# A residual with weights chosen per batch: 4 MB transfers in a ring of four rooms, channel-major weights, one loop per engine

## The reference

```
W = weights[condition]                      # (64, 128, 128)
out = x + einsum('bct,bcd->bdt', x, W)      # for each batch: out = x + W^T x
```

## Time and profile before

| | |
|---|---|
| median of 3 runs | 325.06 us (324.98 to 325.37) |
| profiled execution | 324.97 us, its span 323.2 us |
| TensorE, VectorE, GpSimd busy | 240.3, 146.6, 19.0 us |
| moved by the DMA engines | 135.30 MB, mean 419 GB/s |
| granted clock of TensorE, mean | 0.928 |

### The profile page before, as it was taken

One profiled execution on the slowest core, in us unless ns is written; L12 is line 12 of the kernel. 1 busy time (PEld: TensorE's weight loads), 2 busy tenths in 40 slices (PEclk: granted clock), 3 DMA queues, 4 the chain that ended last, 5 costly groups with the idle time before them and its releaser, 6 DMA issues.

```text
span 323.2 us, 2326 instructions
## 1 busy us (share of the span) xinstructions
PE 240.3 (74%) x512; PEld 101.3 (31%) x512; DVE 146.6 (45%) x64; ACT 0.2 (0%) x1; POOL 19.0 (6%) x69
## 2 busy tenths in 40 slices
PE   0029999999999986867996869866688786878000
PEld 0014444444444432322342323322233332333000
DVE  0003766766757752555173552543545254553200
ACT  0000000000000000000000000000000000000000
POOL 0011100101001000000010000000000000000000
PEclk9999999999999998999597997999899798899755
DMA  7999999999999999999999999999999999999996
GB/s 279 382 414 422 422 425 429 428 424 430 426 428 430 425 431 426 427 431 426 429 428 427 430 425 428 430 425 430 428 427 430 426 429 428 426 430 426 429 430 284
DMA packets 17940, 135.30 MB, mean 419 GB/s; under 512 B 1042, under 2 KB 1042, under 8 KB 1554
## 3 DMA queue, kind: packets, MB, share of 16 engines
q10 hardware_dynamic: 9234, 68.16, 49.9%
q1 hardware_dynamic: 8704, 67.11, 49.7%
HBM read 68.16 MB, written 67.11 MB: 419 GB/s over the span
## 4 chain that ended last, share of the span: by engine, by line
DMA 69%; PE 20%; DVE 2%; issue 1%; ACTq 0%; POOLq 0%; DVEq 0%; ACT 0%; SPq 0%; POOL 0%
DMA out<-x_ring 59%; PE product L114 20%; DMA weight_table<-weights 6%; DMA x_ring<-x 5%; DVE x_ring L138 2%; POOLq L90 0%; ACTq L147 0%; ACTq L145 0%; DVEq L138 0%; ACT weight_table L149 0%; ACTq L144 0%; SPq L72 0%; POOLq L92 0%; SPq L84 0%; POOLq L97 0%
## 5 line engine op out<-in xcount | busy, mean ns | idle before, releaser
L114 PE MATMUL product<-x_ring,chosen_weights 128*128 (+1 forms) x512 | 240.3, 629 | 58.6 <-POOL chosen_weights L92 23.2
L138 DVE TENSOR_TENSOR x_ring<-product,x_ring 128x2048 f32 x64 | 146.6, 2291 | 154.7 <-PE product L114 154.7
L114 PEld LDWEIGHTS product<-x_ring,chosen_weights 128*128 128x128 f32 x512 | 101.3, 201 | 196.7 <-issue 196.7
L92 POOL COPY chosen_weights<-weight_table 128x128 f32 x64 | 18.8, 293 | 243.1 <-issue 125.2
L149 ACT MOVE_SHAPE weight_table<-weights x1 | 0.2, 160 | 1.4 <-PEq L166 1.4
L166 POOL MEMSET const-float32-0.0<- 128x1 f32 x1 | 0.1, 98 | 0.1
L166 POOL MEMSET const-bfloat16-1.0<- 128x1 bf16 x1 | 0.1, 101 | 0.0
L166 POOL MEMSET const-uint8-127<- 128x1 uint8 x1 | 0.1, 101 | 0.0
L166 POOL MEMSET const-float32-1.0<- 128x1 f32 x1 | 0.1, 98 | 0.0
L166 POOL BASE_LOAD x1 | 0.0, 17 | 0.2 <-issue 0.2
## 6 DMA issues: line engine op xcount, KB each, us to landing
x_ring<-x SPq DMA_DIRECT2D x32, 2048.0 KB, 16.3
out<-x_ring ACTq DMA_DIRECT2D x32, 2048.0 KB, 38.6
condition_row<-condition ACTq DMA_DIRECT2D x1, 0.2 KB
weight_table<-weights ACTq DMA_DIRECT2D x1, 0.5 KB, 18.8
```

Of the source, the lines that this page charges most:

```text
L92: pool.tensor_copy(chosen_weights[b][:, :], weight_table[:, bass.ds(state * features, features)]).then_inc(weights_chosen, 1)
L114: last = pe.matmul(product[:, b % psum_slots, m * BANK_COLUMNS:(m + 1) * BANK_COLUMNS], chosen_weights[b][:, :], x_ring[:, bass.ds(ring_co ...
L138: dve.tensor_tensor(tile, product[:, b % psum_slots, :], tile, AluOpType.add).then_inc(sum_done, 1)
```

## The change

The unit of transfer becomes four batches (4 MB). The ring keeps its size and has 4 rooms of 32 KB per partition (2 turns of 2), so two loads and two stores may be in flight. The weights array is transposed on the host to (channel, state, feature), so that each channel's 8 KB lie in one piece; ScalarE issues this load ahead of the condition row. The written-out first turns go: semaphores are given starting amounts instead. `room_free` takes the place of `out_stored`, `psum_free` that of `sum_done`, and a new `weights_free` is raised by VectorE once it has seen a product done; GpSimd waits for it before it overwrites a buffer of chosen weights. The core of the diff:

```diff
-BATCHES = 2
-STEPS = 4
+GROUP = 4
+IN_FLIGHT = 2
 RING_TURNS = 2
...
-            for u in range(STEPS):
-                load(0, u)
-
-            with sp.Fori(1, RING_TURNS) as turn:
-                for u in range(STEPS):
-                    sp.wait_ge(x_loaded[u], 16 * turn)
-                    load(turn, u)
-            with sp.Fori(RING_TURNS, turns) as turn:
-                for u in range(STEPS):
-                    sp.wait_ge(x_loaded[u], 16 * turn)
-                    sp.wait_ge(out_stored[u], 16 * (turn - RING_TURNS + 1))
-                    load(turn, u)
+            for g in range(IN_FLIGHT):
+                sp.sem_inc(x_loaded[g], 16)
+                sp.sem_inc(room_free[g], 16 * RING_TURNS)
+            with sp.Fori(0, turns) as turn:
+                for g in range(IN_FLIGHT):
+                    sp.wait_ge(x_loaded[g], 16 * (turn + 1))
+                    sp.wait_ge(room_free[g], 16 * (turn + 1))
+                    sp.dma_start(ring_group(turn, g), dram_group(x, turn, g)
+                                 ).then_inc(x_loaded[g], 16)
...
-                    pool.wait_ge(product_done, (turn - 1) * (STEPS * BATCHES) + b + 1)
-                    choose(turn, b)
+            pool.sem_inc(weights_free, per_turn)
+            with pool.Fori(0, turns) as turn:
+                for b in range(per_turn):
+                    pool.wait_ge(weights_free, turn * per_turn + b + 1)
...
+            dve.sem_inc(psum_free, psum_slots)
             with dve.Fori(0, turns) as turn:
...
+                    dve.wait_ge(product_done, turn * per_turn + b + 1)
+                    dve.sem_inc(weights_free, 1)
                     dve.tensor_tensor(tile, product[:, b % psum_slots, :], tile,
-                                      AluOpType.add).then_inc(sum_done, 1)
+                                      AluOpType.add).then_inc(psum_free, 1)
...
             act.dma_start(condition_row[0:1, :], condition.rearrange("(o b) -> o b", o=1)
                           ).then_inc(condition_loaded, 16)
-            act.dma_start(weight_table[:, :].rearrange("c (s d) -> c s d", s=states),
-                          weights.rearrange("s c d -> c s d")).then_inc(table_loaded, 16)
...
+            with act.Fori(0, turns) as turn:
+                for g in range(IN_FLIGHT):
+                    act.wait_ge(room_free[g], 16 * (turn + RING_TURNS))
+                    act.wait_ge(psum_free, turn * per_turn + (g + 1) * GROUP + psum_slots)
+                    act.dma_start(dram_group(out, turn, g), ring_group(turn, g)
+                                  ).then_inc(room_free[g], 16)
...
-        "weights": np.ascontiguousarray(L0_cond_weights),
+        "weights": np.ascontiguousarray(np.asarray(L0_cond_weights).transpose(1, 0, 2)),
```

More of the change, by code:

```diff
@@ L26, in conditioned_residual @@
     batches, channels, time = x.shape
-    states, _, features = weights.shape
-    turns = batches // (STEPS * BATCHES)
-    group = BATCHES * time
+    _, states, features = weights.shape
     matmuls = time // BANK_COLUMNS
     psum_slots = PSUM_BANKS // matmuls
+    per_turn = IN_FLIGHT * GROUP
+    turns = batches // per_turn
+    group_columns = GROUP * time
     with ExitStack() as ctx:
@@ L48, in conditioned_residual, with ring_column, ring_group, dram_group @@
         table_loaded = sem("table_loaded")
-        x_loaded = [sem(f"x_loaded{u}") for u in range(STEPS)]
-        out_stored = [sem(f"out_stored{u}") for u in range(STEPS)]
+        x_loaded = [sem(f"x_loaded{g}") for g in range(IN_FLIGHT)]
+        room_free = [sem(f"room_free{g}") for g in range(IN_FLIGHT)]
+        weights_free = sem("weights_free")
         weights_chosen = sem("weights_chosen")
         product_done = sem("product_done")
[L54 to L65, removed]
+        psum_free = sem("psum_free")
+        def ring_column(turn, g):
+            return (turn % RING_TURNS) * (IN_FLIGHT * group_columns) + g * group_columns
+        def ring_group(turn, g):
+            return x_ring[:, bass.ds(ring_column(turn, g), group_columns)].rearrange(
+                "c (b t) -> c b t", b=GROUP)
+        def dram_group(tensor, turn, g):
+            return tensor[bass.ds(turn * per_turn + g * GROUP, GROUP)].rearrange("b c t -> c b t")
         block = ctx.enter_context(nc.Block())
@@ L70, in _ @@
         def _(sp):
-            def load(turn, u):
-                sp.dma_start(ring_group(turn, u), batches_of(x, turn, u)).then_inc(x_loaded[u], 16)
-            for u in range(STEPS):
-                load(0, u)
-            with sp.Fori(1, RING_TURNS) as turn:
-                for u in range(STEPS):
-                    sp.wait_ge(x_loaded[u], 16 * turn)
-                    load(turn, u)
-            with sp.Fori(RING_TURNS, turns) as turn:
-                for u in range(STEPS):
-                    sp.wait_ge(x_loaded[u], 16 * turn)
-                    sp.wait_ge(out_stored[u], 16 * (turn - RING_TURNS + 1))
-                    load(turn, u)
+            for g in range(IN_FLIGHT):
+                sp.sem_inc(x_loaded[g], 16)
+                sp.sem_inc(room_free[g], 16 * RING_TURNS)
@@ L96, in _ @@
             pool.wait_ge(condition_loaded, 16)
             pool.wait_ge(table_loaded, 16)
[L98 to L101, removed]
-                    pool.wait_ge(product_done, (turn - 1) * (STEPS * BATCHES) + b + 1)
-                    choose(turn, b)
+            pool.sem_inc(weights_free, per_turn)
+            with pool.Fori(0, turns) as turn:
+                for b in range(per_turn):
+                    pool.wait_ge(weights_free, turn * per_turn + b + 1)
+                    state = pool.value_load(condition_row[0:1, bass.ds(turn * per_turn + b, 1)],
+                                            min_val=0, max_val=states - 1)
+                    pool.tensor_copy(chosen_weights[b][:, :],
+                                     weight_table[:, bass.ds(state * features, features)]
+                                     ).then_inc(weights_chosen, 1)
@@ L106, in _ @@
         @block.tensor
         def _(pe):
[L108 to L128, removed]
+            with pe.Fori(0, turns) as turn:
+                for b in range(per_turn):
+                    g, within = divmod(b, GROUP)
+                    if within == 0:
+                        pe.wait_ge(x_loaded[g], 16 * (turn + 2))
+                    pe.wait_ge(weights_chosen, turn * per_turn + b + 1)
+                    pe.wait_ge(psum_free, turn * per_turn + b + 1)
+                    for m in range(matmuls):
+                        last = pe.matmul(
+                            product[:, b % psum_slots, m * BANK_COLUMNS:(m + 1) * BANK_COLUMNS],
+                            chosen_weights[b][:, :],
+                            x_ring[:, bass.ds(ring_column(turn, g) + within * time + m * BANK_COLUMNS,
+                                              BANK_COLUMNS)],
+                            start=True, stop=True)
+                    last.then_inc(product_done, 1)
@@ L157, in _ @@
-            for u in range(STEPS):
-                act.wait_ge(out_stored[u], 16 * turns)
+            with act.Fori(0, turns) as turn:
[4 more added lines that the diff above has]
+                                  ).then_inc(room_free[g], 16)
+            for g in range(IN_FLIGHT):
+                act.wait_ge(room_free[g], 16 * (turns + RING_TURNS))
```

16 lines of the change are left out of this document (7 added, 9 removed).

## The result

The changed kernel took 329.5 us in the median of 4 runs (328.56 to 330.60), the kernel before 325.22: a ratio of 1.0123, 95% interval [1.0102, 1.0144].

A forecast was written before the change was run, and what follows sets the result against it. The DMA engines, pushing 135.3 MB plus losses at both ends, were taken as the bound. With -2.1 us weights, -1.8 trickle and +5.3 idle, span 324.6 plus 1.8 outside gave 326.4 us against 325.0; range 322.8 to 329.6.

The forecast's parts named there:

- an idle stretch ahead of a lone last store: Near the end: DMA engines stand idle from 308.6 to 313.9 us, 5.3 us, before the last 4 MB store runs alone.
- rival 3: Middle: four rooms are too few, so the load stream pauses in every group; 329.2 us, chance 0.09.
- Weights, -2.1 us: Start: channel-major weights with 8 KB runs give back the whole 2.1 us lost at 377 GB/s; bounds 0 and 2.1.
- Rival 2: Start: the weights bring nothing and everything behind shifts by 2.1 us; 328.5 us, chance 0.09.
- TensorE's start 15.5 us: Start: TensorE's first matmul moves from 21.84 to 15.5 us, which by itself buys nothing.
- First store issued 34.6, first packet 38.2: First group: its store is issued at 34.6 us after the fourth add, with its first packet 3.6 us later.
- Loops and semaphores, 0: All turns: initial increments and merged loops cost 0, hidden under the transfers; bounds -0.5 to +0.5 us.
- Load 4's first packet 58.3: First turn: load 4 waits for the first store to land at 54.7 us, then 3.6 us to its first packet.
- Last load landed 294.4: End of the load stream: at 19.6 us a pair, load 15 ends at 293.5 and lands at 294.4 us.
- The last group, 18.1 us from its first matmul to its last add's end: Tail: four batches computed from 294.7 to 312.8 us, including +1.7 for TensorE's clock, bounds 0 and 2.8.
- First packet of the last store +1.1, then 9.8 us, 0.9 to the end: Tail: last store starts on idle DMA engines at 313.9 us, ends at 323.7, span ends at 324.6; start bound 3.6.
- Rival 1: End: last group covered, DMA engines never idle, only the weights' 2.1 us go; 322.9 us, chance 0.20.

The follow-up runs named there:

- e5: Changed kernel with only the last group's store split into four pieces of one batch, each issued behind its own add: 323.96 us, ratio 0.9954.
- e7: Changed kernel with a fifth room in the ring and the loops written out, still 4 MB transfers: 323.56 us, ratio 0.9945.
- e2: Kernel before with only the weights changed to channel-major, loaded in one piece per channel: 324.15 us, ratio 0.9949.
- e1: Changed kernel with transfers of 2 MB again (GROUP 2, IN_FLIGHT 4): 324.24 us, ratio 0.9954.
- e9: Changed kernel with transfers of one batch, 1 MB (GROUP 1, IN_FLIGHT 8): 326.22 us, ratio 1.0025.
- e6: Changed kernel with 22 small extra matmuls on TensorE before each group's wait for its load: 326.69 us, ratio 1.0048.
- e3: Changed kernel with the old state-major weights load (runs of 512 B): 330.59 us, ratio 1.0144.
- e8: Changed kernel with the loops written out and still four rooms, a control for five rooms: 328.14 us, ratio 1.0103.

## Why the prediction was right, and where its sizes were off

The forecast was 326.4 us (span 324.6), slower by an idle stretch ahead of a lone last store. That stretch is what happened, in the place and for the reason given: e5 and e7 take it away and with it the loss. The size was short: +1.4 us forecast, +4.0 measured (0.0123 x 325.2; 3.3 to 4.7 by the interval). The measured 329.5 lies inside the range by 0.1 us, and that is luck: my forecast by itself went only to 329, and the range reached further for the rivals, whose highest, 329.2, was rival 3's pauses in the middle, and they didn't come. By the steps, on the profiled execution:

- **Weights, -2.1 us:** -1.7 (e2). The 2.1 counted the slow start as the weights' too; the stretch in which they run explains 1.1. Rival 2 is out. The Trainium skill ("DMA: Bandwidth & Descriptors", Specifications) puts the smallest transfer for full rate at 512 B; the trace doesn't agree: 392 GB/s with 512-byte runs beside x, 425 with 8 KB (5.9 to 19.6 us, e2).
- **TensorE's start 15.5 us:** 15.95. **First store issued 34.6, first packet 38.2:** issued 34.69, first packet 38.3. **Loops and semaphores, 0:** 0 (e1 against e2).
- **Load 4's first packet 58.3:** 59.7, +1.4; in the trace the load queue has no packet from 52.1 to 59.7 us. The wait from its issue to its first packet was as forecast (issued at 55.92, 3.7 us), so the issue was 1.2 late. 0.7 of that is the head: I let the DMA engines run at 422 GB/s from 1.9 to 38.2 us, and they ran at 414. What is missing stands at the very start, where the weights ran alone, x being issued at 1.57 and having its first packet only at 5.0. The other 0.5 isn't accounted for. The stretch to 38.2 us, and the DMA view from 1.8 to 4.9 us:

```profile
1.90:38.20 36.30, 22.25 (x48) 9.84 (x49) 11.46 (x5) 3.81 (x13) 1.00 0.99 414
```

```profile
DMA packets 124, 1.02 MB, mean 328 GB/s; under 512 B 0, under 2 KB 0, under 8 KB 0
```

- **Last load landed 294.4:** 296.89, +2.5. 1.4 is load 4's. The rest comes from an uneven end. For load 4 the 16 packets of 4 bytes that end a load (see e9) lie within 0.35 us (78.99 to 79.33), for the last load within 1.94 us (294.46 to 296.40). The DMA view of either stretch, 78.9 to 79.4 and 294.4 to 296.5 us (16 packets under 512 B in each):

```profile
DMA packets 43, 0.22 MB, mean 442 GB/s; under 512 B 16, under 2 KB 16, under 8 KB 16
...
DMA packets 126, 0.90 MB, mean 429 GB/s; under 512 B 16, under 2 KB 16, under 8 KB 16
```

In between, the first of the 16 comes every 19.59 us, as forecast, and the last of them falls behind by 1.6 us over the eleven loads. The landing came 0.5 us behind the last packet where I had 0.9 (-0.4), and the rest is rounding. I had let a load end like the mean of its bytes.
- **The last group, 18.1 us from its first matmul to its last add's end:** 316.73 - 297.22 = 19.5, +1.4. I priced the clock at +1.7 with a bound of 2.8. Here the first add came 6.92 us after the first matmul (297.22 to 304.14); in e6, at full clock, 3.93 us (296.31 to 300.24): the clock cost 3.0 us. The whole group at full clock takes 16.5 (e6), as I had it. TensorE idled 3.10 us before its last group, longer than the 2.8 of the kernel before. But a longer idle time alone doesn't lengthen the loss: in e3 and e8 it idled 4.21 and 4.00 us and the group took 15.69 and 15.70 us of matmuls, 1.7 above full clock. The difference is how much of the group runs at half clock. First the changed kernel, whose group began at 297.22 with the clock already down, then e3, whose group began at 298.93 at full clock (the third number from the end of the row is the granted clock):

```profile
296.50:303.20 6.70, 5.98 (x7) 2.52 (x8) 0.15 (x1) 0.00 (x0) 0.50 1.01 428
...
299.40:302.70 3.30, 3.30 (x5) 1.35 (x4) 0.00 (x0) 0.00 (x0) 0.00 (x0) 0.50 0.99 417
```

Some 6.0 us at half clock cost 3.0, some 3.4 us cost 1.7. What decides between the two stays open; it may also be the source of the spread of 2 us over the four runs, which wasn't tried.
- **First packet of the last store +1.1, then 9.8 us, 0.9 to the end:** the DMA engines are nearly idle to 317.8, which is 1.1 after the add; then 11.0 us to the end of the span instead of 10.7, +0.3.

2.5 + 1.4 + 0.3 = 4.2 us is the difference of the spans, 328.8 - 324.6. The term most mis-sized is the end of the last load: I gave it bounds below (load 4 earlier) and none above. The clock came out slightly above its bound (3.0, bound 2.8), the last store inside its own.

Rival 1 (the last group covered, 322.9) didn't happen here; five rooms and the split store bring the kernel near it (323.6 and 324.0). Rival 3 (pauses in every group) is out: 426 to 429 GB/s in every slice of the middle.

## What to carry to other kernels

When the DMA engines are the bound and the next transfer is always queued, look for no gain from a bigger one in the middle (here 427, 428 and 428 GB/s with 1, 2 and 4 MB); it lengthens the serial chain behind the last load: compute on the whole group, then a store of the whole group. Ask whether the backlog of stores at that moment is longer than this chain; if not, split the last store, or give the ring one more room. Walk the streams through the first turn, since the one pause there sets how late the last load is. And count the end of a transfer by the slowest of the DMA engines that carry it, not by its bytes.

## What the runs showed of the hardware that I had not expected

- The first packet of a queue came about 1 us after its issue when the DMA engines were idle (before: x 1.1; changed: weights 1.0, last store 0.9), and 2.4 to 4.3 us after when the other queue kept them busy (before: weights 4.3, first store 3.7; changed: x behind the weights 3.5, first store 3.6, load 4 3.7; x behind the weights in e1 3.2, in e3 2.5, in e9 2.4).
- The 16 DMA engines don't keep step: the ends of one load lay 0.35 us apart for load 4 and 1.94 us for load 15 in the changed kernel, 1.7 us in the middle of e1 and 4.3 us in e9, and the last load landed 0.5 us behind the last of them.
- 22 extra matmuls per group of four batches, 5.1 us of TensorE's time, took 2.4 us off the kernel (e6).
- Transfers of 1 MB were slower than 2 MB, by 0.7% (1.0025 against 0.9954), at both ends and not in the middle.
